# A graph layer and a routed expert layer on one core: the masks' lead over the sums, the expert weights' queue and the set-up's order are changed

## The reference

```python
def gnn(x, adj, ...):                       # x is the layer-normed input
    mask = (adj > 0).astype(x.dtype)
    deg = jnp.sum(mask, axis=1, keepdims=True)
    agg = mask @ x / jnp.maximum(deg, 1.0)
    combined = jnp.concatenate([x @ W_self + b_self, agg @ W_nb + b_nb], axis=-1)
    return relu(combined @ W_comb + b_comb)

def ffn(x, ...):                            # 8 experts, each row goes to 2
    topk_scores, topk_idx = top_k(x @ Wg + bg, 2)
    topk_w = softmax(topk_scores)
    h = gelu(einsum('nd,edh->neh', x, W1) + b1)
    y = einsum('neh,ehf->nef', h, W2) + b2
    return sum over the 2 chosen of topk_w * y

x = x + gnn(layernorm(x), adj, ...)
x = x + ffn(layernorm(x), ...)
```

## Time and profile before

| | before |
|---|---|
| median of 3 runs | 525.07 us (524.85 to 525.54) |
| span of the profiled execution | 521.0 us (the runs' times also hold what lies around the span, so they are 3.9 to 4.5 us longer) |
| PE, DVE, ACT, POOL busy | 85%, 71%, 49%, 59% of the span |
| bytes moved by DMA | 122.47 MB, mean 235 GB/s |

### The profile page before, as it was taken

How to read it: one execution, slowest core, us unless ns; L and a number is a source line. 1 busy time by engine, 2 the same in 40 slices (tenths; PEclk the granted TensorE clock), 3 DMA queues, 4 the chain that set the end, 5 groups by cost and what they waited for, 6 DMA issues and landing times.

```text
span 521.0 us, 12708 instructions
## 1 busy us (share of the span) xinstructions
PE 444.2 (85%) x4162; PEld 380.2 (73%) x4162; DVE 370.7 (71%) x1056; ACT 257.6 (49%) x403; POOL 305.2 (59%) x346
## 2 busy tenths in 40 slices
PE   4599989999999999989799899745999999997720
PEld 3388878888888888768688688633887778876610
DVE  2889744858758888679587798662677777679982
ACT  2558660543634354344354342330677777776630
POOL 2679778244355766756567563676255556555570
PEclk9789999999999999989999899965799999999975
DMA  8999898599999999999999931964555555588665
GB/s 247 267 264 270 239 243 221 147 278 258 256 272 277 298 306 307 299 297 276 301 282 307 291 132 62 275 230 153 166 164 164 164 161 153 149 325 335 195 211 161
DMA packets 49167, 122.47 MB, mean 235 GB/s; under 512 B 11081, under 2 KB 20173, under 8 KB 48080
## 3 DMA queue, kind: packets, MB, share of 16 engines
q1 hardware_dynamic: 31632, 68.29, 47.2%
q0 software_dynamic: 16080, 50.49, 32.4%
q10 hardware_dynamic: 1392, 2.88, 1.9%
HBM read 96.52 MB, written 26.93 MB: 237 GB/s over the span
## 4 chain that ended last, share of the span: by engine, by line
PE 27%; DVE 21%; DMA 19%; issue 12%; ACT 6%; SPq 6%; POOL 5%; another core or an unknown queue 2%; DVEq 1%; ACTq 0%; POOLq 0%
DMA wst<-in_L_ffn_W_dram 11%; PE bank L1326 7%; PE bank L1346 7%; PE bank L1227 6%; SPq L440 5%; POOL stage L563 3%; DMA x_sb<-in_x_dram 2%; DMA stage<-in_adj_dram 2%; PE bank L1218 2%; PE bank L1219 2%; DMA stage<-in_adj_dram,gidx 2%; PE bank L1313 2%; DVE stage L1112 2%; DVE mask L820 2%
## 5 line engine op out<-in xcount | busy, mean ns | idle before, releaser
L1218 PE MATMUL bank<-z_flat,maskT 128*128 128x257 f16 x1024 | 231.6, 277 | 0.7 <-issue 0.4
L1219 PE MATMUL bank<-z_lo,maskT 128*128 128x256 f16 x1024 | 231.5, 276 | 0.0
L642 POOL DMA_INDIRECT pair_out<-rows,enum x78 | 79.6, 1021 | 66.9 <-DVE gate L1125 29.7
L563 POOL DMA_INDIRECT stage<-in_adj_dram,gidx x64 | 76.0, 1188 | 64.3 <-ACT mask L667 52.0
L1218 PEld LDWEIGHTS bank<-z_flat,maskT 128*128 128x128 fp8e4 x1024 | 101.4, 99 | 14.2 <-issue 0.5
L1219 PEld LDWEIGHTS bank<-z_lo,maskT 128*128 128x128 fp8e4 x1024 | 101.4, 99 | 13.0 <-issue 0.3
L574 POOL DMA_INDIRECT dispatched<-rows,slot x64 | 65.9, 1030 | 39.5 <-issue 20.2
L710 ACT ACTIVATE xh<-x_sb,nb,rs 128x256 f32<-128x256 f32 x32 | 19.2, 600 | 139.6 <-POOL nb L631 139.6
L667 ACT ACTIVATE mask<-stage,m 128x2048 fp8e4<-128x2048 int32 x32 | 64.0, 2001 | 15.2 <-DVE maskT L827 7.5
L1346 PE MATMUL bank<-w,stage 128*128 x468 | 60.7, 281 | 8.2 <-DVE stage L1112 4.3
L1326 PE MATMUL bank<-stage,w 128*128 128x256 f16 x468 | 61.4, 284 | 6.2 <-DVE stage L1098 4.4
(11 more groups left out here) (175 smaller groups left out, 586.0 us busy)
## 6 DMA issues: line engine op xcount, KB each, us to landing
stage<-in_adj_dram SPq DMA_DIRECT2D x256, 128.0 KB
stage<-dispatched SPq DMA_DIRECT2D x39, 260.0 KB
wst<-in_L_ffn_W_dram SPq DMA_DIRECT2D x16, 256.0 KB
z_lo<-pair_out SPq DMA_DIRECT2D x4, 1024.0 KB
dispatched<-pad SPq DMA_DIRECT2D x15, 260.0 KB
out_dram<-x_sb SPq DMA_DIRECT2D x28, 128.0 KB
maskT<-pair_out SPq DMA_DIRECT2D x3, 1024.0 KB, 8.5
x_sb<-in_x_dram ACTq DMA_DIRECT2D x6, 256.0 KB, 8.5
```

The lines of the kernel that those rows point to most:

```text
L563: gp.indirect_dma_start(out=stage[:, s, b - 2, :], out_offset=None, in_=adj_q[:, :], in_offset=bass.IndirectOffsetOnAxis(ap=gidx[:, 0:1], ...
L642: gp.indirect_dma_start(out=yp_dram[:, :], out_offset=bass.IndirectOffsetOnAxis(ap=enum[:, a, s:s + 1], axis=0), in_=ysb[:, a, s, :], in_o ...
L1218: mm(acc[u % 2][:, 0:D + 1], a, z_hi[:, i, :], start=(i == 0), stop=False)
L1219: last = mm(acc[u % 2][:, 0:D], a, z_lo[:, i, :], start=False, stop=(i == NT - 1))
```

## The change

There are four parts.

1. **The set-up.** On DVE, `fold_max` and its chain no longer stand behind the statistics of tiles 4 to 11: `stats(1)` moves between the two maxima, `stats(2)` behind the split of `wf`. ACT normalises tiles 4 to 7 behind `wf`. Only pairs 0 and 1 are transposed before the loop over pairs; the function `zt_behind` puts pairs 2 and 3 behind pair 0, 4 behind 1, 5 and 6 behind 2, 7 and 8 behind 3, and i + 5 behind i from then on.
2. **The masks.** Five are made amid the row products (behind pairs 1, 4, 7, 10, 13). Step 0 makes tile 5's. Steps 3 to 9 make the mask three tiles ahead, steps 11 to 15 two ahead, steps 17 to 30 one ahead (`made_in`); steps 10 and 16 make none. Transposes are dealt out by themselves (`turned_in`): steps 3 to 16 turn the mask of tile s + 1, step 17 none, from step 18 on that of tile s, and they now stand behind lo2 in DVE's step, not ahead of it. POOL's gathers go with `made_in`, two tiles further.
3. **The expert weights.** `load_expert` leaves SP's queue for ACT's: expert 0 behind the loop over pairs, expert k + 1 at the end of ACT's step 4k + 5, behind its mask, where ACT waits for `expert_lo(k)` of DVE.
4. **PE's sum of the expert maxima** moves from between the halves of step 4k + 2 to behind the second half.

The diff, cut to its core:

```diff
+        def zt_behind(i):
+            return [j for j in {0: (2, 3), 1: (4,), 2: (5, 6), 3: (7, 8)}.get(i, (i + AHEAD,)) if j < PAIRS]
...
-        MASKS, HELD, MADE = (1, 3, 6, 8, 10, 12), 4, 2
+        MASKS, HELD = (1, 4, 7, 10, 13), 4
+        def made_in(s):
+            if s == 0:
+                return len(MASKS)
+            for first, end, ahead in ((3, 10, 3), (11, 16, 2), (17, NT - 1, 1)):
+                if first <= s < end:
+                    return s + ahead
+            return None
+        def turned_in(s):
+            if 3 <= s <= 16:
+                return s + 1
+            return s if 18 <= s < NT else None
...
-                if t == len(MASKS):
-                    load_expert(0)
-                if t >= B + HELD + 1 and t % B == 1:
-                    load_expert((t - HELD - 1) // B)
-            load_expert(E - 1)
...
-            self_and_const(0)
+            for k in range(3):
+                self_and_const(k)
             gather(6)
-            self_and_const(1)
-            self_and_const(2)
-            gather(7)
...
-                if HELD <= s < NT - 2 - MADE:
-                    gather(s + 2 + MADE)
+                m = made_in(s)
+                if m is not None and m + 2 < NT:
+                    gather(m + 2)
...
+            def load_expert(k):
+                if k:
+                    act.wait_ge(s_el, 2 * k)
+                for w, m in enumerate((W1, W2)):
+                    act.dma_start(wst[:, w], m[k].rearrange("(t p) n -> p t n", p=P)).then_inc(s_ew, 16)
...
-            for k in range(OWN // B):
-                normalise(k)
-            for i in range(AHEAD - 1):
-                zt_hi(i)
+            normalise(0)
+            zt_hi(0)
+            zt_hi(1)
...
-            zt_hi(AHEAD - 1)
+            normalise(1)
...
-                if HELD <= known < NT - MADE:
-                    masks(t + MADE, u + MADE, known + MADE)
+                m = made_in(t)
+                if m is not None:
+                    masks(m, m, m)
+                if t >= ESPLIT and (t - ESPLIT) % B == 0 and (t - ESPLIT) // B < E - 1:
+                    load_expert((t - ESPLIT) // B + 1)
...
             stats(0)
-            stats(1)
-            stats(2)
             fold_max(0)
             dve.wait_ge(s_small, 16)
             v.tensor_reduce(fmx[:, 1:2], wg_f[:, :, :].rearrange("p t n -> p (t n)"), AX.X, ALU.max, apply_absolute_value=True).then_inc(s_fmx, 1)
+            stats(1)
...
-            v.tensor_scalar(wg_s[:, 0], wg_f[:, :, :], scw[:, 1:2], None, ALU.mult).then_inc(s_wf, 1)
-            dve.wait_ge(s_wf, 1)
...
+            stats(2)
+            v.tensor_scalar(wg_s[:, 0], wg_f[:, :, :], scw[:, 1:2], None, ALU.mult).then_inc(s_wf, 1)
+            dve.wait_ge(s_wf, KT + 1)
+            v.scalar_tensor_tensor(wg_s[:, 1], wg_f[:, :, :], scw[:, 1:2], wg_s[:, 0], ALU.mult, ALU.subtract).then_inc(s_wf, 1)
...
-            for i in range(2, AHEAD):
-                zt_lo(i)
             stats(3)
...
-                if HELD <= known < NT:
-                    mask_transpose(t, u, known)
...
+                m = turned_in(t)
+                if m is not None:
+                    mask_transpose(m, m, m)
...
-                if HELD <= known < NT - MADE:
-                    masks(t + MADE, u + MADE, known + MADE)
+                m = made_in(t)
+                if m is not None:
+                    masks(m, m, m)
...
-            for i in range(3):
-                z_transpose(i)
+            z_transpose(0)
+            z_transpose(1)
...
-            for i in range(3, AHEAD):
-                z_transpose(i)
...
                     neighbours(u, 0, known == 0)
+                    neighbours(u, 1, known == 0).then_inc(s_mm, 1)
                 if u % B == PM and PM <= known < NT + PM:
                     k = div(t, u, known, PM, B)
                     pe.wait_ge(s_emx, k + 1)
...
-                if live(known, 0):
-                    neighbours(u, 1, known == 0).then_inc(s_mm, 1)
...
-            pe.wait_ge(s_wf, KT + 2)
+            pe.wait_ge(s_wf, KT)
...
-                if i + AHEAD < PAIRS:
-                    z_transpose(i + AHEAD)
+                for j in zt_behind(i):
+                    z_transpose(j)
```

More of the change, by code:

```diff
@@ L440, in load_adj @@
                         sp.dma_start(stage[Q * g:Q * g + Q, s, b, :], adj_v[t // B, t % B, g, :, b, :]).then_inc(s_adj[s], 16)
-            def load_expert(k):
-                if k:
-                    sp.wait_ge(s_el, 2 * k)
-                for w, m in enumerate((W1, W2)):
-                    sp.dma_start(wst[:, w], m[k].rearrange("(t p) n -> p t n", p=P)).then_inc(s_ew, 16)
             def write_dummy(i):
@@ L631, in _ @@
                     gp.tensor_scalar(nb2[:, t:t + 1], mv2[:, t % B, 0:1], rs[:, t:t + 1], -1.0, ALU.mult, ALU.mult).then_inc(s_nb2, 1)
-                for _ in range(1 if s < NT - 2 - MADE else 2):
+                for _ in range(1 if s < NT - B else 2):
                     if sent < B * ((s - SLOT + (s == LAST_POWERS - 1)) // B + 1):
@@ L696, in _ @@
                 sc.activation(rows_f[:, at(2 * i, 2), 0:D], pair(sps[i % 2]), ACT.Copy, scale=scw[:, 2:3]).then_inc(s_self, 1)
-                if i + AHEAD < PAIRS:
-                    zt_hi(i + AHEAD)
+                for j in zt_behind(i):
+                    zt_hi(j)
                 if i in MASKS:
@@ L701, in _ @@
                     masks(t, t, t)
+            load_expert(0)
             def main_step(t, u, known):
@@ L883, in _ @@
                                        ALU.mult, ALU.subtract).then_inc(s_ul, 1)
-                if i + AHEAD < PAIRS:
-                    zt_lo(i + AHEAD)
+                for j in zt_behind(i):
+                    zt_lo(j)
                 if i in MASKS:
@@ L1289, in _ @@
                     last.then_inc(done, 1)
-                if i + AHEAD < PAIRS:
-                    z_transpose(i + AHEAD)
+                for j in zt_behind(i):
+                    z_transpose(j)
                 if i == 8:
                     const_product()
+            pe.wait_ge(s_wf, KT + 2)
             pe.wait_ge(s_cst, 5)
```

1 line of the change is left out of this document (removed).

## The result

The changed kernel takes 545.59 us (median of 4 runs, 543.13 to 551.44), the kernel before 525.31 beside it: a ratio of 1.0372, interval 1.0323 to 1.0421. It is slower by 3.7%, where I had forecast 1.1% faster. The profiled executions have spans of 541.4 and 521.0 us, 20.4 us apart, and it is these that I take apart. In every run whose span is on record the time is 1.7 to 1.9 us longer than the span, so the 3.9 to 4.5 us that I read off for the kernel before are not what lies around its span: its profile must be of an execution of about 522.8 us, faster than any of its four timed ones. The forecast isn't touched by it, as it goes by the difference.

The account below looks back on a forecast made before the run. A ring of ACT and POOL, slightly slower than PE, was taken as the bound. Terms summed to -3.8 us at the 26th tile, 5.7 us at PE's end: 519.4 us (own range 516 to 523; overall 510 to 527).

Parts of the forecast that it names:

- First turn: Start of the main loop: first tile normalised at 88.0 in place of 91.1 us, 3.1 of the set-up's 4.8 arriving.
- Steps 4 to 9: Main loop: masks three tiles ahead wait for their own step's transpose behind lo2; +5.0 us, bounds 0 and +7.8.
- Set-up: Before the main loop: earlier maxima, more transposes, no wait for z_lo; 4.8 us earlier, main loop starting at 73.5.
- the ring: Main loop: ACT's mask, POOL's gather and reciprocal deviation, ACT's next normalising; a turn of 7.56 to 8.34 us holds PE.
- Steps 10 and 16: Main-loop steps without a mask: no gather, turn bound by DVE at 6.5 us; 1.8 and 1.2 us off.
- Weights: Main loop: expert loads no longer behind adj transfers in SP's queue; -8.1 us, bounds 0 and -10.8.
- ACT's new wait: End of ACT's steps 4k + 5, waiting for expert_lo: turns of 8.6 against 8.34 us, +1.5 in all.
- Transpose behind lo2: DVE's main-loop steps: sum reading and slots come 1.2 us later; 0.8 for each of four steps, +3.2 us.
- The end stretch: Behind the 26th tile's wait, three sums and the experts: 186 us, not touched by the edits.
- the early steps don't pay: Rival, steps 4 to 9: transposes already late before, so the +5.0 falls away; 509.5 to 514 us, chance 0.20.
- ACT held by DVE: slower: Rival, end of ACT's steps 4k + 5: late expert_lo costs 2.2 us more each, five count; 530.4 us, chance 0.18.

Follow-up runs that it names:

- e1: Changed kernel with DVE's mask transposes put back ahead of lo2; ratio 1.0077 to the kernel before.
- e8: e1 with each of POOL's additions cut to one column of 256, so the output is incomplete; ratio 0.9994 to the kernel before.
- e14: e8 with the five set-up masks at row products 1, 3, 6, 8, 10; ratio 0.9885 to the kernel before.
- e19: Changed kernel with the set-up masks at row products 1, 3, 6, 8, 10, transposes still behind lo2; ratio 1.0272 to the kernel before.
- e4: Kernel before with only the expert weights' loads moved to ACT's queue; ratio 0.9971 to the kernel before.
- e13: e11 with the expert weights back in SP's queue; ratio 1.0578 to the kernel before.
- e11: e1 with gather 6 behind one addition and gather 7 ahead of the last five; ratio 1.0057 to the kernel before.
- e9: Changed kernel with transposes ahead of lo2 in steps 3 to 9 alone; ratio 1.0243 to the kernel before.
- e23: Changed kernel unaltered, run on e22's chip; ratio 1.0401 to the kernel before.
- e22: The mended kernel: changed kernel with transposes ahead of lo2 and set-up masks at row products 1, 3, 6, 8, 10; ratio 0.996 to the kernel before.

## Why the prediction was wrong

It failed in *First turn* and in *Steps 4 to 9*, and in both DVE and POOL held each other, which no term and no rival of mine contained; in the first, POOL's own list (additions, then two gathers, ahead of the reciprocal deviation) did the rest. For tile 25 I had 3.8 us earlier, and it came 14.9 later: of these 18.7 us the first turn makes 12.0, steps 4 to 9 make 4.2, and the turns behind them 2.5. Another 2.5 arise before the last sum ends and 4.9 behind it.

- *Set-up*, 4.8 us earlier: 1.6 (first sum at 76.7 against 78.3). The first row product started at 21.32, not at 20, as it waited 4.05 us for DVE's halves; the 1.9 us of z_lo did go, but PE then waited 1.82 for the constant's product. The transposes' 0.44 each was right.
- *First turn*, 88.0: 100.0. This is the largest miss, 12 us. I priced the ring from a mask's start and took POOL and the data as ready. I had put at nothing, without a reason, the additions that the change moves ahead of gathers 6 and 7, and the loads that the set-up masks start. By e1, e8 and e14: additions 6.8 us at the first tile, late masks 2.0 there once the additions are gone. e19 shows that the two are nearly one: with the masks early and all additions kept, the first tile comes at 92.3, 7.7 us sooner, while steps 4 to 9 stay as they were (56.5 us).
- *Steps 4 to 9*, +5.0 (upper bound 7.8): +9.2. The +1.3 for the mask was measured (2.8 against 1.47); the term was mis-sized by the gather that now always falls under DVE's mask, 2.07 against 1.47 us, and by the two steps with expert halves, which grew to 9.5 like the others and not by 0.1.
- *Steps 10 and 16*, -1.8 and -1.2: -2.2 (turn of 6.15) and -1.4 (6.3). Right.
- *Weights*, -8.1: DVE's wait went from 10.8 to 4.3, PE's from 9.9 to 1.0. But the queue is not what did it by itself: e4 shows nothing on the old order, and in e1, on the same queue with shorter turns, DVE waits 10.7 us again. So part of the fall came from a slower loop, which asks for weights less often. e13 shows that the order of masks of e11 would lose 2.4 to 5% without the queue; on the changed kernel itself this was not run. I took a gain for what was a condition. The Trainium skill's rule that I set against the edit ("DMA: Bandwidth & Descriptors", "Issuing engines are not separate DMA queues") agrees with e4 (ratio 0.9971); e13 shows that the issuing engine still matters, by when it comes to the load.
- *ACT's new wait*, turns of 8.6: 8.8 (tiles 10, 18, 22). Right; the rival made of it, which asked for turns over 10 us, had no part.
- *Transpose behind lo2*, +3.2 by tile 25: e9 against e1, which differ in this alone, 3.1. The size came out by luck: not four turns grew by 0.8 us, but most turns by 0.1 to 0.7 (that of tile 8 to 8.17 from 7.57), while the waits for weights moved: the turn of tile 21 fell to 8.20 from 11.34, that of tile 25 rose to 10.90 from 7.75. By e23 and e22, which differ in the masks' places too, it is 6.6. Besides, the last tile is normalised 7.6 us after the last sum in place of 4.9, which "not touched by the edits" left out.
- *The end stretch*, 186 us: 191.0. 2.7 are the last tile's; 2.2 are not explained (PE is 1.4 us longer busy in this stretch, at a mean granted clock of 0.86 against 0.87, which may be a part). On e22's chip the two kernels differ there by 1.6.
- The rivals: *the early steps don't pay* was wrong in its sign. *ACT held by DVE: slower* had the right sign by luck: its mechanism had no part.

What would have shown it: the DVE instruction of 2.38 us at 86.58 in the trace before, almost six times its usual length, next to five additions of POOL.

## What to carry to other kernels

When a change moves a step, list for every engine what it passes, POOL's arithmetic first: long runs of POOL additions must end before DVE is needed (in e22 they only moved to where they cost less), and a gather should not start just behind a DVE conversion. Look in the old trace for single instructions that take a multiple of their usual time, since they mark an overlap that a reordering can make larger. Loads are started by what frees their buffer: moving that later in a phase with time to spare is a cost in the next phase. And a part that is worth nothing alone may be what keeps another part from losing.

## What the runs showed of the hardware

- One 128x256 DVE instruction with two SBUF inputs was held 7.28 us, in e11 10.35, over a row of POOL's additions, from its start until the whole row had ended; DVE got no turn between two additions. A conversion from int32 to fp8 (1.23 us) was held to 6.19, in e19 to 8.65. Not held by the same row, in the trace after: a DVE transpose (84.00, its usual 1.25 us) and an instruction with one tile from PSUM and one from SBUF (85.66, its usual 0.48).
- An indirect DMA's issue on POOL takes 0.94 us alone and up to 2.08 beside that conversion: it ended 0.1 us after the conversion where it had started first (1.47 us at 126.62 before), and 0.8 to 0.9 after it where it had started second (2.07 at 114.57 after).
- A load of one expert's weights, of the same size each time, landed 3.6 us after its issue in the mended kernel's set-up (81.2 to 84.8) and 21.6 us in e8 (76.1 to 97.7), both from ScalarE's queue, so the queue alone doesn't set its time. The DMA engines were busy for a share of 0.55 of 80 to 86 us there, and 1.03 of 76 to 98 us in e8; but in e14 the load took 6.6 us (76.8 to 83.4) at 1.06, so how full they are doesn't set it alone either.
